# A graph attention layer on one core: the limits of every pair copied on chip, and group 0 started in halves

## The reference

```python
h = relu(layernorm(x))
xs, xd = h @ W_src.T, h @ W_dst.T                      # per head
alpha = leaky(sum(xs[src] * att_src[type]) + sum(xd[dst] * att_dst[type]))
a = softmax of alpha over the edges of each dst        # 8 heads
out = segment_sum(xs[src] * a * edge_weight, dst) + bias
z = layernorm(out + h) * g1 + b1
ff = gelu(z @ W1.T + b1f) @ W2.T + b2f                 # 256 -> 1024 -> 256
result = x + layernorm(z + ff) * g2 + b2
```

## Time and profile before

| what | value |
|---|---|
| median of 3 runs | 3072.69 us (3071.02 to 3077.78) |
| profiled execution, own time | 3058.6 us |
| its span | 3056.8 us |
| mean granted clock of TensorE | 0.968 |
| PE, DVE, ACT, POOL busy | 92%, 75%, 59%, 72% of the span |
| first record of the sum stage | 443.68 us |
| last record | at about 536 us |
| first gather of group 0's records | 548.79 us |
| first FFN product of group 0 | 566.23 us |

### The profile page before, as it was taken

One profiled execution on the slowest core, in us unless ns is written; L12 is line 12 of the kernel. 1 busy time (PEld: TensorE's weight loads), 2 busy tenths in 40 slices (PEclk: granted clock), 3 DMA queues, 4 the chain that ended last, 5 costly groups with the idle time before them and its releaser, 6 DMA issues.

```text
span 3056.8 us, 55232 instructions
## 1 busy us (share of the span) xinstructions
PE 2813.9 (92%) x18391; PEld 2564.6 (84%) x18391; DVE 2300.0 (75%) x6038; ACT 1798.0 (59%) x3180; POOL 2208.6 (72%) x1687
## 2 busy tenths in 40 slices
PE   2777738699999999999999999999999999999998
PEld 2777626599999999999999999999999999999998
DVE  3766667477777777777777777777777777777776
ACT  2655526366666666666666666666666666666664
POOL 6555365677777777777777777777777777777773
PEclk9888869799999999999999999999999999999999
DMA  5333247455555555555555555555555555555551
GB/s 143 113 119 121 86 112 235 110 148 146 145 145 146 145 145 145 145 145 145 146 146 146 146 146 147 147 148 146 147 146 146 146 146 147 145 147 146 147 136 62
DMA packets 596303, 429.44 MB, mean 140 GB/s; under 512 B 430425, under 2 KB 532991, under 8 KB 596020
## 3 DMA queue, kind: packets, MB, share of 16 engines
q1 hardware_dynamic: 563476, 347.53, 39.2%
q0 software_dynamic: 31424, 77.33, 12.7%
q10 hardware_dynamic: 1120, 1.05, 0.1%
HBM read 247.16 MB, written 178.66 MB: 139 GB/s over the span
## 4 chain that ended last, share of the span: by engine, by line
PE 80%; POOL 1%; DVE 0%; issue 0%; DMA 0%; ACT 0%; SPq 0%; DVEq 0%; POOLq 0%; ACTq 0%
PE ps_f L1476 36%; PE ps_x L1515 9%; PE ps_t L1493 6%; PE ps_a L1493 6%; PE ps_t L1492 6%; PE ps_t L1491 6%; PE ps_a L1492 6%; PE ps_a L1491 6%; ACT arena L876 0%; DMA arena<-z_rows 0%; POOL arena L705 0%; POOL arena L723 0%; DMA arena<-sums,node_rows 0%; POOL zt_lo L743 0%; POOL arena L735 0%
## 5 line engine op out<-in xcount | busy, mean ns | idle before, releaser
L856 ACT ACTIVATE act_hi<-ps_f,hidden_bias 128x512 fp32r<-128x512 f32 x784 | 538.4, 687 | 919.1 <-PE ps_f L1476 918.9
L1339 DVE TENSOR_TENSOR act_lo<-ps_f,act_hi 128x512 fp32r<-128x512 f32 x784 | 539.4, 688 | 468.7 <-ACT ps_f L857 457.3
L1476 PE MATMUL ps_f<-zt_hi,ffn_hi 128*128 128x512 f32 x1568 | 623.1, 397 | 7.2 <-DVE act_lo L1339 5.6
L1476 PE MATMUL ps_f<-zt_lo,ffn_hi 128*128 128x512 f32 x1568 | 620.0, 395 | 0.0
L1476 PE MATMUL ps_f<-zt_hi,ffn_lo 128*128 128x512 f32 x1568 | 619.8, 395 | 0.0
L857 ACT ACTIVATE ps_f<-ps_f,hidden_bias 128x512 f32<-128x512 f32 x784 | 513.0, 654 | 0.0
L705 POOL DMA_INDIRECT arena<-sums,node_rows x391 | 405.0, 1036 | 111.9 <-issue 92.5
L1493 PE MATMUL ps_a<-ffn_hi,act_lo 128*128 128x256 f32 x1568 | 438.3, 280 | 0.0
L1491 PE MATMUL ps_a<-ffn_hi,act_hi 128*128 128x256 f32 x1568 | 437.6, 279 | 0.0
L1492 PE MATMUL ps_a<-ffn_lo,act_hi 128*128 128x256 f32 x1568 | 437.2, 279 | 0.0
L1493 PE MATMUL ps_t<-ffn_hi,act_lo 128*128 128x256 f32 x1560 | 436.1, 280 | 0.0
(11 more groups left out here) (245 smaller groups left out, 6614.8 us busy)
## 6 DMA issues: line engine op xcount, KB each, us to landing
xb<-in_x SPq DMA_DIRECT2D x97, 512.0 KB, 5.0
z_rows<-arena SPq DMA_DIRECT2D x97, 512.0 KB
arena<-z_rows SPq DMA_DIRECT2D x388, 128.0 KB
out<-arena SPq DMA_DIRECT2D x97, 512.0 KB, 4.5
h_rows<-h SPq DMA_DIRECT2D x96, 512.0 KB
arena<-h_rows SPq DMA_DIRECT2D x384, 128.0 KB, 3.7
msgs<-arena SPq DMA_DIRECT2D x49, 256.0 KB
arena<-msgs SPq DMA_DIRECT2D x49, 256.0 KB
```

Of the source, the lines that this page charges most:

```text
L856: act.activation(act_hi[:, m % AB, :], ps_f[:, m % 2, :], ACT.Gelu, bias=hidden_bias[:, m:m + 1]).then_inc(act_hi_ready, 1)
L1339: dve.tensor_tensor(act_lo[:, m % AB, :], ps_f[:, m % 2, :], act_hi[:, m % AB, :].bitcast(F32), ALU.subtract).then_inc(act_lo_ready, 1)
L1476: ins = pe.matmul(ps_f[:, m % 2, 0:cols], ffn1[a][:, k, m * P:(m + 1) * P], zt[b][:, i.par, k, 0:cols], start=(j == 0), stop=(j == 3 * KC ...
```

## The change

The two DMAs that copy a pair's limits on chip are issued for all 49 pairs instead of the last four; `load_ends` is gone. For pairs 0 to 47 they count on the pair's `agg_stored` semaphore, which so rises by 48 per pair instead of 16; only pair 48's count on `fix_in`. DVE waits for them ahead of the fix. The first two gathers of group 0 count on a semaphore of their own, `rec_first`, and DVE adds and takes the statistics of these two tiles before it waits for the other two (`first_lift`). Tiles 2 and 3 of group 0 are normalised on DVE (`first_tiles`), tiles 0 and 1 on ACT; `turn_z` and `first_residual` wait for both. The numbers of POOL's pacing stay as they are. The diff without the lists of semaphores:

```diff
@@ -94,7 +94,6 @@
 SB = 20
 SBN = 6
 RO = 4
-ENDS_KEPT = 4
 SPLITS = 9
 NB = 4
 TURN_AT = (1, 8)
...
@@ -348,19 +347,13 @@
         def records_stored(eng):
 
             for i in range(RO):
-                eng.wait_ge(agg_stored[i], 16 * ((NPAIR + RO - 1 - i) // RO))
+                eng.wait_ge(agg_stored[i], 48 * ((NPAIR + RO - 1 - i) // RO) - 32 * ((NPAIR - 1) % RO == i))
 
         def loaded(j):
 
             b = j.off % SB
             return msg_soon[:, 2 * b:2 * b + 2, :] if b < SBN else msg_late[:, 2 * (b - SBN):2 * (b - SBN) + 2, :]
 
-        def load_ends(eng, c):
-
-            to = 2 * (NPAIR - ENDS_KEPT)
-            eng.dma_start(fix_ends[c:to:2, :, :], sums[0:EP].rearrange("(j p c) d -> c j p d", p=P, c=2)[c][0:NPAIR - ENDS_KEPT, 0:P:P - 1, :]).then_inc(fix_in, 16)
-
-
         def by_quarter(a):
 
             return a.rearrange("p (q b f) -> p q b f", q=QS, b=KC)
...
@@ -372,6 +365,10 @@
         def acc(i):
 
             return ps_a if i.par == 0 else ps_t
+
+        def rec_count(g, groups):
+
+            return 64 * groups - 32 * (g.par == 0)
 
         def tiles(g):
 
...
@@ -561,15 +558,9 @@
                 if not j.exists(NPAIR):
                     return
                 b = 2 * (j.off % RO)
-                if j.n == NPAIR - 1:
-                    for k in range(NPAIR - ENDS_KEPT - RO, NPAIR - ENDS_KEPT):
-                        sp.wait_ge(agg_stored[k % RO], 16 * (k // RO + 1))
-                    for c in range(2):
-                        load_ends(sp, c)
                 sp.wait_ge(rec_made, j.n + 1)
-                if j.n >= NPAIR - ENDS_KEPT:
-                    for c in range(2):
-                        sp.dma_start(fix_ends[2 * j.n + c:2 * j.n + c + 1, :, :], rec_out[0:P:P - 1, b + c, :]).then_inc(fix_in, 16)
+                for c in range(2):
+                    sp.dma_start(fix_ends[2 * j.n + c:2 * j.n + c + 1, :, :], rec_out[0:P:P - 1, b + c, :]).then_inc(fix_in if j.n == NPAIR - 1 else agg_stored[j.off % RO], 16)
                 sp.dma_start(sums[0:EP].rearrange("(j p c) d -> j p c d", p=P, c=2)[j.n],
                              rec_out[:, b:b + 2, :]).then_inc(agg_stored[j.off % RO], 16)
             steps(sp, sum_pair, 1 - SB, NPAIR, *SUM_LOOP)
...
@@ -697,13 +688,13 @@
 
 
             def gather_records(g):
-                wait_count(pool, rec_in[g.par], 64 * g.half)
+                wait_count(pool, rec_in[g.par], rec_count(g, g.half))
                 wait_count(pool, y_made, 2 * (g.n - 1))
                 pool.sem_inc(pool_gate, 1)
                 for t in range(tiles(g)):
                     at = node_rows[:, TG * g.n + t:TG * g.n + t + 1]
                     pool.indirect_dma_start(rec[:, g.par, t, :], None, sums,
-                                            bass.IndirectOffsetOnAxis(ap=at, axis=0)).then_inc(rec_in[g.par], 16)
+                                            bass.IndirectOffsetOnAxis(ap=at, axis=0)).then_inc(rec_first if g.n == 0 and t < 2 else rec_in[g.par], 16)
 
             def first_rstd(n):
                 pool.wait_ge(y_prepared, 2 * n.n + 2)
...
@@ -724,6 +715,8 @@
 
             def first_residual(n):
                 pool.wait_ge(z_ready, n.n + 1)
+                if n.n == 0:
+                    pool.wait_ge(z_half, TG // 2)
                 wait_count(pool, u_ready, 2 * (n.n - 1))
                 if n.n == 0:
                     for t in range(TG):
...
@@ -871,7 +864,7 @@
                 wait_count(act, zt_turned, KC * min(n.n, 1))
                 wait_count(act, z_stored, 16 * (n.n - 1))
                 wait_count(act, res_part, n.n)
-                for t in range(TG):
+                for t in range(TG if n.n else TG // 2):
                     to, of = z[:, t, :], y[:, t, :]
                     ins = act.activation(by_half(to) if n.n == 0 else to, by_quarter(of) if n.n == 0 else of, ACT.Identity, bias=y_shift[:, t:t + 1],
                                          scale=y_rstd[:, t:t + 1])
...
@@ -1235,7 +1228,7 @@
             def record(j):
 
                 dve.wait_ge(agg_done, j.n + 1)
-                wait_count(dve, agg_stored[j.off % RO], 16 * j.before(RO))
+                wait_count(dve, agg_stored[j.off % RO], 48 * j.before(RO))
                 dve.tensor_tensor(rec_out[:, 2 * (j.off % RO):2 * (j.off % RO) + 2, :], ps_a[:, j.par, :].rearrange("p (c d) -> p c d", c=2),
                                   wide(rows[:, 0:1, :], [P, 2, D]), ALU.add).then_inc(rec_made, 1)
 
...
@@ -1251,16 +1244,28 @@
 
             def lift_add(n):
                 wait_count(dve, z_ready, n.n)
-                dve.wait_ge(rec_in[n.par], 64 * n.half + 16 * tiles(n))
+                dve.wait_ge(rec_in[n.par], rec_count(n, n.half) + 16 * tiles(n))
                 dve.sem_inc(dve_gate, 1)
                 for k in range(2):
                     dve.wait_ge(lifted, TG * n.n + 2 * k + 2)
                     dve.tensor_tensor(y[:, 2 * k:2 * k + 2, :], ps_x[:, k, :].rearrange("p (t d) -> p t d", t=2),
                                       rec[:, n.par, 2 * k:2 * k + 2, :], ALU.add).then_inc(y_made, 1)
 
+            def first_lift():
+                n = Step(0, 0, 4)
+                dve.sem_inc(dve_gate, 1)
+                for k in range(2):
+                    dve.wait_ge(*((rec_first, 32) if k == 0 else (rec_in[0], 32)))
+                    dve.wait_ge(lifted, 2 * k + 2)
+                    dve.tensor_tensor(y[:, 2 * k:2 * k + 2, :], ps_x[:, k, :].rearrange("p (t d) -> p t d", t=2),
+                                      rec[:, 0, 2 * k:2 * k + 2, :], ALU.add).then_inc(y_made, 1)
+                    dve.wait_ge(y_made, k + 1)
+                    for t in (2 * k, 2 * k + 1):
+                        dve.bn_stats(y_stat[:, t, :], y[:, t, :]).then_inc(y_stats, 1)
+
             def first_stats(n):
                 dve.wait_ge(y_made, 2 * n.n + 2)
-                for t in range(TG):
+                for t in range(TG if n.n else 0):
                     dve.bn_stats(y_stat[:, t, :], y[:, t, :]).then_inc(y_stats, 1)
                 dve.wait_ge(y_stats, 2 * TG * n.n + TG)
                 dve.sem_inc(dve_gate, 1)
...
@@ -1270,6 +1275,12 @@
                 wait_count(dve, y_scaled, n.n)
                 dve.tensor_scalar(y_var, y_mv[:, :, 1], EPS, None, ALU.add).then_inc(y_prepared, 1)
                 dve.tensor_scalar(y_mm, y_mv[:, :, 0], -1.0, None, ALU.mult).then_inc(y_prepared, 1)
+
+            def first_tiles():
+                dve.wait_ge(y_scaled, 1)
+                for t in range(TG // 2, TG):
+                    dve.tensor_scalar(by_half(z[:, t, :]), by_quarter(y[:, t, :]), y_rstd[:, t:t + 1], y_shift[:, t:t + 1],
+                                      ALU.mult, ALU.add).then_inc(z_half, 1)
 
             def turn(n, landed, of, to, turned):
 
...
@@ -1343,9 +1354,11 @@
                 o, n, a, g = i - 1, i + 1, i + 2, i + 3
                 back, on, norm, front = o.exists(NG), i.exists(NG), n.exists(NG), a.exists(NG)
                 if norm and not on:
-                    lift_add(n)
+                    first_lift()
                 if norm:
                     first_stats(n)
+                if norm and not on:
+                    first_tiles()
                 if norm and not on:
                     z_rest(n)
                     lift_add(a)
...
@@ -1382,7 +1395,9 @@
                 if on:
                     act_rest(i, 7)
             steps(dve, sum_pair, 0, NPAIR + 1, *SUM_LOOP)
-            dve.wait_ge(fix_in, 16 * (2 + 2 * ENDS_KEPT))
+            dve.wait_ge(fix_in, 32)
+            for i in range(RO):
+                dve.wait_ge(agg_stored[i], 48 * ((NPAIR + RO - 2 - i) // RO))
             dve.tensor_tensor(fix_ends[C, 1, :], fix_ends[C, 1, :], rows[C, 0, :], ALU.subtract).then_inc(fix_step, 1)
             dve.wait_ge(fix_pe, 1)
             dve.tensor_tensor(fix_rec[C], ps_a[C, 0, 0:D], fix_ends[C, 0, :], ALU.add).then_inc(fix_made, 1)
...
@@ -1519,6 +1534,8 @@
 
             def turn_z(n, front):
                 pe.wait_ge(z_ready, n.n + 1)
+                if n.n == 0:
+                    pe.wait_ge(z_half, TG // 2)
                 pe.wait_ge(nt_lo, KC * (n + front).n + KC)
                 for k in range(KC):
                     for t in range(TG):
```

More of the change, by code:

```diff
@@ L311, in build @@
          n_stats, n_prepared, n_pow, n_scaled, nh_ready, nt_turned, nt_hi, nt_lo, lifted,
-         y_made, y_stats, y_prepared, y_pow, y_scaled, z_ready, zt_turned, zt_hi, zt_lo,
+         y_made, y_stats, y_prepared, y_pow, y_scaled, z_ready, z_half, rec_first, zt_turned, zt_hi, zt_lo,
          x_res_ready, res_part, res_ready, f_done, act_hi_ready, act_f_ready, act_lo_ready, act_used,
@@ L323, in build @@
          n_stats n_prepared n_pow n_scaled nh_ready nt_turned nt_hi nt_lo lifted
-         y_made y_stats y_prepared y_pow y_scaled z_ready zt_turned zt_hi zt_lo
+         y_made y_stats y_prepared y_pow y_scaled z_ready z_half rec_first zt_turned zt_hi zt_lo
```

## The result

| what | before | after |
|---|---|---|
| median beside each other | 3070.41 us (17 runs) | 3079.80 us (17 runs) |
| ratio, 95% interval | | 1.0035 (1.0028 to 1.0042), +10.7 us |
| profiled execution, span | 3056.8 us | 3077.6 us |
| first weighing (L1232; after L1225) | 433.17 us | 445.65 us |
| record 5 | 461.57 us | 475.97 us |

The kernel is slower, and by more than the 0.2% that can be told. Only ratios within one set of runs are used: the kernel before has 3070.41 us beside after, and 3061.65 to 3063.02 beside the kernels of the experiments.

The account below looks back on a forecast made before the run. Took SP's queue, filled by 90 added copies, to bound the sum stage: +7.4 there, -1.3 for halved records, -1.0 for normalisation on two engines, +5.1 us on 3072.7, giving 3077.8 us; range 3067 to 3091.

Parts of the forecast that it names:

- The forecast's case: Sum stage: SP's issue of the added copies sets the pace; +5.1 us in all, own range +2.9 to +9.1, chance 0.72.
- SP bounds the sum stage: Sum stage: from pair 5 SP needs 2.20 us a pair with a load, 1.70 without, against 1.74 and 1.62 now.
- +8.3 by the page: End of sum stage: loss if the last copy landed 0.9 us later, by the skill page's 2.0 us DMA cost.
- The fix: DVE's step opening the join: would start at 549.7 in place of 542.24 us, +7.4 us.
- The join: Chain after the sums, up to PE's transposes: halves of group 0's records gain 1.3 us, normalisation on two engines 1.0.
- on two engines: Group 0's normalisation: ACT does two tiles instead of four, 2.08 becoming 1.05 us, DVE two beside it; -1.0 us.
- up to pair 5 the loop is slower than SP would be, and nothing is lost: Start of the sum stage, up to pair 5's store at 462.30 us: the added copies cost nothing there.
- everything that comes later keeps its length: After PE's last wait at about 608 us: lengths unchanged, so time won or lost earlier shows fully at the end.
- B: Sum stage: PE drops to 1.2 GHz in the drawn-out loop; +18 us, 3091, or +12 for half the stage; chance 0.10.
- C: Sum stage: SP has slack, so only the gains remain; -4.2 us, 3068.5; chance 0.12.
- rival D: Join: its gains don't come while SP still bounds the sum stage; +8 us; chance 0.06.
- The feared late landing: Sum stage: one DMA landing late, like the 3.69 us pair 47's record waits now, could raise the loss to +15.

Follow-up runs that it names:

- join_only: The kernel before with only the halves of group 0's records and its normalisation on two engines, limits as before; 3062.21 us beside 3063.02.
- couples: After, with two copy DMAs for two pairs in place of four, on semaphores of their own; 3070.77 us beside 3063.02 for the kernel before.
- limits_only: The kernel before with only the on-chip copies of all pairs' limits, join unchanged; 3078.71 us beside 3063.02.
- loads_on_act: After, with the message loads from the 20th pair on issued by ACT; 3073.16 us beside 3063.02 for the kernel before.
- one_of_two: limits_only with one copy per pair for pairs 0 to 47, even chunks' limits left out; 3070.39 us beside 3061.87 for the kernel before.
- limits_ro6: limits_only with six record buffers in place of four; 3074.38 us beside 3061.65 for the kernel before.
- couples_ro6: limits_only with two copy DMAs for every two pairs, six record buffers and three semaphores; 3072.37 us beside 3061.87 for the kernel before.
- dummy_issues: The kernel before plus two 4-byte DMAs per pair in SP's queue for pairs 0 to 44, nobody waiting; 3066.47 us beside 3061.65.
- kept24: The kernel before with ENDS_KEPT = 24: limits copied on chip for pairs 25 to 48, read back for 0 to 24; 3068.86 us beside 3061.87.
- early_load: join_only with ENDS_KEPT = 6 and the reading back issued at pair 47 instead of 48; 3068.94 us beside 3061.87 for the kernel before.

## Why the prediction was right and where it failed

**The forecast's case came.** 3077.8 was forecast and 3079.8 measured, but part of that is luck with the base: 3072.7 was the median of three runs, and that of 17 is 3070.4. The difference is the honest number: +5.1 forecast, +9.4 between the medians and +10.7 by the ratio, about twice the forecast, with +8.3 of it seen in the profiles. "Within 0.2%" had the larger chance (0.47) and "slower" (0.43) came.

**SP bounds the sum stage: right, and well sized.** From pair 5's to pair 48's copies 85.1 us were forecast and 84.9 measured; SP's pair is 2.14 and 1.66 (2.20 and 1.70). The copy takes as long under full traffic as in the earlier trace rows. The last landing came 1.05 us behind the end of its issue (562.72 to 563.77), 1.61 behind the start, as the row of before had it. The Trainium skill (DMA: Bandwidth & Descriptors, Anatomy of one DMA) gives a fixed cost of some 2.0 us. That section describes DMAs issued by GpSimd, while this copy is SP's; the time measured here is lower and decides, so the prediction's +8.3 by the page fell away. The fix: +7.4 forecast, +7.1 from record 5 on.

**The join: right.** From the last gather to the power -1.2 (forecast -1.3), on two engines -1.0 (-1.0); two tiles took DVE 0.73, less than ACT's 1.10. Another 0.6 came at POOL, whose first gather now starts 5.97 us after the fix in place of 6.55. In join_only both gains stand in the profile, too, but not in the medians.

**The step that failed: "up to pair 5 the loop is slower than SP would be, and nothing is lost".** It was 1.9 us here, and it is no chance of one profile: with one or two copies per pair, from the first pair on, this part takes 29.8 to 30.3 us in six kernels, and 26.0 to 28.8 in the seven whose first pairs have none. (couples, 27.9, is the exception.) The step from record 4 to 5 alone takes 3.9 to 4.9 us in those seven and 5.4 to 6.2 in all seven with copies there; SP's queue has gaps at that point. Why, the runs don't show. The second term missed is "everything that comes later keeps its length": +0.6 up to PE's last wait and +1.4 behind it. Behind it the same work began at a lower clock (windows of 13 us from the end of the wait, after and then before, the first number in brackets being PE's matmuls):

```profile
627.07:640.07 13.00, 13.00 (x69) 11.84 (x70) 11.08 (x23) 8.13 (x13) 11.60 (x9) 0.77 0.45 122
```

```profile
607.70:620.70 13.00, 13.00 (x79) 11.84 (x80) 12.06 (x25) 8.08 (x13) 11.70 (x9) 0.88 0.48 126
```

PE worked all 13 us both times; 0.11 of the clock less over 13 us is 1.4 us at full speed. Other profiles agree: from the same wait to the end eight kernels with 0.87 or 0.88 in this window take 2449.0 to 2449.2 us, and the five with 0.77 to 0.83 (after, limits_only, couples, loads_on_act, one_of_two) take 2449.6 to 2450.5. limits_ro6, with 0.87 and 2450.1, doesn't fit. By the profiles the sum is +1.9 + 7.1 - 2.8 + 0.6 + 1.4, unrounded +8.3.

**The reason was right and incomplete.** SP's queue is full in after's loop from pair 5 on, and its pieces add up to the loop's length. But the forecast took for granted that with SP relieved the loop would be that of before. Four kernels say no: with SP busy for 55 to 63 of 82 to 86 us it is as slow or nearly so (couples, couples_ro6, loads_on_act), and with half of the rows it loses 3 to 4 us, at the edge of what single profiles tell (one_of_two; SP busy for 55.7 us, while dummy_issues with 50.8 keeps the pace of before in its profile). kept24 fits both readings. The time goes with the number of rows copied (8 to 16, 86 to 90, 168 to 176 rows: 73 to 76, 78 to 79, 82 to 86 us) and not with SP's time; one_of_two, couples and couples_ro6 issue 42 to 44 copies each and take 78.9, 82.4 and 85.0. A second limit of about the same height lies behind the first. Its place is seen: longer stops at few points of the loop, in couples_ro6 with DVE and ACT both waiting for PE. Its cause stays open. It was not told apart whether the copies hold up the DMA queues, the memory's ports, the loading of the program or something else that PE needs.

**The rivals.** B (PE loses its clock) did not come in the loop: the granted clock there is 0.93 (0.94 before) although PE works for only 34.5 of 49 us; in stretches of 10 us from 471 to 551 it is 0.83 to 1.00.

```profile
471.00:520.00 49.00, 34.46 (x162) 26.30 (x161) 31.42 (x57) 28.43 (x75) 24.30 (x24) 0.93 0.81 224
```

The prediction cited a kernel of the Trainium skill (TensorE: Matmul & The Clock Gate, A second HAM failure mode: psum-queue depth-cycling) whose clock swings through short idle pieces. Here the clock is no lower than before: 0.94 over 476 to 562, where before's loop has 0.90 over 462 to 541. C (the copies don't bind) is out by SP's timeline, the prediction's rival D by the join. The feared late landing did not come either: DVE's longest wait for a buffer is 2.5 us.

**Also open**: the stage ahead of the first weighing. It is the same code in all kernels and took 433 to 437 us in both profiles of before, couples_ro6 and loads_on_act, and 439 to 446 in the ten others. Ratio and profile would agree better if the edited kernels mostly started the sums some 4 us later than before does (an estimate from the differences given ahead of the experiments). Then part of the ratio of after, too, would be the program's layout, theory E, and 8.3 the price of its change. But beside after the kernel before had itself 3070.4 us, some 8 more than in the other sets. Whether a program or the chip or place that it got decides that was not tried.

No kernel here beats the one before by more than the measurement tells; join_only is level with it.

## What to carry to other kernels

Before small DMAs are added to a loop, write out the timeline of the queue that issues, piece by piece: it gave the time of 43 pairs here within 0.3%, and a copy of two rows costs its queue more than a store of 256 KB (0.57 us against 0.40). But a bound worked out for one resource is a floor: take it away in an experiment (fewer issues, another engine, half of the data) before believing that it is the only price. And a transfer moved earlier, to get it out of the way, may meet traffic that was over by the time it had before.

## What the runs showed of the hardware

- The issue of a DMA on SP's queue depends on its form more than on its size: 4 bytes 0.25 us, two rows of 1 KB from two partitions 0.57, four rows from one partition 0.60, a store of 256 KB 0.32, and 0.40 right behind another issue. On ACT's queue the 256 KB load is 0.33 (0.43 on SP's).
- Behind the reading back of 172 rows from HBM, with four stores issued in the 6 us before it, the next two copies took 4.50 us to issue in place of 1.28 (early_load, one profile).
- A copy of two rows on chip lets the instruction that waits for it start 1.04 to 1.09 us behind the end of its issue (before, after, limits_only, join_only, limits_ro6, one_of_two, couples).
- Some stops of the written-out loop lie at the same pair in every kernel: from record 11 to 12 all 14 profiles have 3.3 us, where the shortest steps are 1.2 to 1.4.
